# Decoder layer on one core: the first keys of cross-attention made earlier, the ranks behind the next queries

## The reference

```
x = layernorm(x + self_attention(x))        # 16 heads of 16; features normalised, then squared scores, causal
x = layernorm(x + cross_attention(x, ctx))  # 8 heads of 64, softmax over 1601 keys, output projection + bias
x = layernorm(x + experts(x))               # 8 experts, top 2 by softmax of a gate, silu(x w1) * (x w3) -> w2
```

## Time and profile before

| | us |
|---|---|
| median of 3 runs | 1288.47 |
| profiled execution | 1291.7 |
| its span, first to last instruction | 1290.0 |
| granted TensorE clock, mean | 0.97 |

### The profile page before, as it was taken

One profiled execution on the slowest core, in us unless ns is written; L12 is line 12 of the kernel. 1 busy time (PEld: TensorE's weight loads), 2 busy tenths in 40 slices (PEclk: granted clock), 3 DMA queues, 4 the chain that ended last, 5 costly groups with the idle time before them and its releaser, 6 DMA issues.

```text
span 1290.0 us, 18849 instructions
## 1 busy us (share of the span) xinstructions
PE 1172.4 (91%) x6456; PEld 685.7 (53%) x6456; DVE 725.9 (56%) x1297; ACT 592.1 (46%) x1031; POOL 715.3 (55%) x617
## 2 busy tenths in 40 slices
PE   3789797879999999999999999999999999999991
PEld 2456464545555555555555555555554466566661
DVE  7686867662466744657835556835665654423222
ACT  5676767624445643545543545444443423222222
POOL 2284656325587775678785776875766132422222
PEclk9899999979999999999999999999998999999996
DMA  6009700001000000100000100000003742332324
GB/s 200 17 9 337 254 2 1 1 1 26 1 1 1 26 1 2 42 1 1 26 34 1 43 1 26 9 26 17 1 1 130 262 103 43 74 45 46 47 37 143
DMA packets 38926, 65.75 MB, mean 51 GB/s; under 512 B 4129, under 2 KB 31393, under 8 KB 38561
## 3 DMA queue, kind: packets, MB, share of 16 engines
q1 hardware_dynamic: 25792, 49.45, 12.0%
q0 software_dynamic: 7152, 9.38, 4.4%
q10 hardware_dynamic: 5888, 5.72, 1.7%
HBM read 50.96 MB, written 30.61 MB: 63 GB/s over the span
## 4 chain that ended last, share of the span: by engine, by line
PE 74%; DVE 15%; issue 4%; ACT 4%; DMA 2%; ACTq 1%; another core or an unknown queue 0%; POOL 0%; SPq 0%; DVEq 0%; POOLq 0%
PE PS L1896 16%; PE PS L1907 12%; PE PS L1783 10%; PE PS L1973 9%; DVE mxp L1511 5%; PE PS L1991 5%; PE PS L1802 3%; PE PS L227 3%; PE PS L1694 2%; PE PS L1704 2%; PE PS L228 2%; PE PS L229 2%; PE PS L1683 2%; PE PS L1982 1%; PE PS L1877 1%
## 5 line engine op out<-in xcount | busy, mean ns | idle before, releaser
L732 POOL TENSOR_TENSOR acc<-acc,PX 128x1024 f32<-128x1024 f32 (+1 forms) x165 | 392.9, 2381 | 127.5 <-ACT PX L1012 118.8
L1012 ACT ACTIVATE PX<-PS 128x1024 f32<-128x1024 f32 (+1 forms) x208 | 212.5, 1026 | 261.9 <-PE PS L1896 256.3
L1511 DVE TENSOR_REDUCE mxp<-PS 128x2 f32<-128x804 f32 x256 | 243.1, 990 | 127.1 <-PE PS L1802 126.2
L1907 PE MATMUL PS<-PX,V 128*64 128x512 f32 (+1 forms) x832 | 209.4, 613 | 0.2 <-ACT PX L1012 0.2
L787 POOL DMA_INDIRECT Y<-yb,goal_u x39 | 60.8, 1558 | 183.6 <-DVE yb L1600 144.2
L1973 PE MATMUL PS<-W,XBT 128*128 x312 | 147.1, 594 | 1.6 <-issue 0.8
L664 POOL TENSOR_SCALAR_AFFINE_SELECT A<-A 128x128 f32<-128x128 f32 x256 | 85.4, 350 | 111.2 <-ACT A L899 108.3
L899 ACT ACTIVATE A<-PS 128x512 f32<-128x512 f32 (+3 forms) x256 | 97.7, 445 | 65.0 <-PE PS L1694 63.8
L1896 PE MATMUL PS<-QH,KH 64*128 64x512 f32 (+1 forms) x416 | 102.3, 488 | 4.8 <-ACT PX L1012 3.2
L1896 PEld LDWEIGHTS PS<-QH,KH 64*128 64x128 f32 (+1 forms) x416 | 38.1, 179 | 117.9 <-issue 81.3
L1907 PEld LDWEIGHTS PS<-PX,V 128*64 128x64 f32 (+1 forms) x832 | 48.6, 137 | 79.1 <-issue 73.2
(11 more groups left out here) (293 smaller groups left out, 2105.5 us busy)
## 6 DMA issues: line engine op xcount, KB each, us to landing
W<-in_w SPq DMA_DIRECT2D x24, 512.0 KB, 4.8
XB<-XG ACTq DMA_DIRECT2D x39, 130.0 KB, 2.1
X<-in_x SPq DMA_DIRECT2D x1, 2048.0 KB, 12.0
Y<-X SPq DMA_DIRECT2D x4, 512.0 KB, 3.4
X<-Y SPq DMA_DIRECT2D x4, 512.0 KB, 5.5
out<-X SPq DMA_DIRECT2D x8, 256.0 KB, 2.1
xt_raw<-in_xt SPq DMA_DIRECT2D x3, 512.0 KB, 3.9
c_raw<-in_ctxt SPq DMA_DIRECT2D x6, 200.0 KB, 2.7
```

The costliest lines, as they stand in the source:

```text
L732: ins = pool.tensor_tensor(sums[0:r], sums[0:r], PX[0:r, (NL * p + t) % NP, :, :], ALU.add)
L1012: act.activation(PX[0:r, u % NP, :, :], PS[0:r, score_buffer(u):score_buffer(u) + 2, :], ACT.Exp, scale=XD ** -0.5)\
L1511: dve.tensor_reduce(mxp[:, p % 2, :, v % NT, v // NT:v // NT + 1].rearrange("p a o -> p (a o)"), PS[:, k:k + 2, 0:BW], AX, ALU.max)\
L1907: mm = pe.matmul(PS[rows, 4, :], V[0:LROWS[j], j, P * p + XD * half:P * p + XD * half + XD], PX[0:LROWS[j], u % NP, half, :], start=(j == ...
```

## The change

The slots of the last batch are filled anew. Each entry of `MEANWHILE` is now three lists: for TensorE behind the second score, ahead of the value products, and behind them.

| step | slot before | slot after |
|---|---|---|
| xt 0, xt 1, q | 5, 6, 7 | 2, 3, 4 (ahead of the values) |
| k 0 to 3 | 9, 10, 11, 12 | 5, 6, 7, 8 |
| v 0 | 13 | 9 |
| max 0 to 11 | two each in 10 to 15 | two each in 9 to 14 |
| max 12 | handover | 15, behind the values |
| max 13 | handover, other banks | handover, banks 0 and 1 |

The context splits stay in slots 1 to 4. VectorE and ScalarE take the same steps in the new order; in slot 15 VectorE now copies the quad ahead of the maximum. The keys of pair 0 can no longer overlap the buffers that are live at slot 5, so high and low keys are laid out by parity of the pair: K0 (even pairs) over `c_first`, K1 (odd pairs) behind the queries, PX behind V. Since K0 lies over `c_first`, the keys of batch 0 wait for all four context splits. In `ROUTING` ranks and settle 0 move from (2, 12) to (3, 1), behind the next "q" and the pair's "total", "hout" and "ctx 3".

```diff
-        PX = sxx("PX", [P, NP, 2, T])
+        K0 = sxx("K0", [P, 2, L], f32r)
         QH, QL = sxx("QH", [P, 2, T], f32r), sxx("QL", [P, 2, T], f32r)
-        KH, KL = sxx("KH", [P, 2, L], f32r), sxx("KL", [P, 2, L], f32r)
+        K1 = sxx("K1", [P, 2, L], f32r)
+        KH, KL = ([K[:, part, :] for K in (K0, K1)] for part in range(2))
         unit = sxx("unit", [P, P], f32r)
         V = sxx("V", [P, NL, INNER])
+        PX = sxx("PX", [P, NP, 2, T])
...
-        sf("under_px", [P, 4096])
...
-                   (2, 12): [("ranks",), ("settle", 0)], (3, 2): [("settle", 1)], (3, 3): [("settle", 2)], (3, 4): [("settle", 3)],
+                   (3, 1): [("ranks",), ("settle", 0)], (3, 2): [("settle", 1)], (3, 3): [("settle", 2)], (3, 4): [("settle", 3)],
...
-        EARLY_MAX = 12
+        EARLY_MAX = 14
...
-        MEANWHILE = {n: [("ctx", n - 1)] for n in range(1, 1 + NB)}
-        MEANWHILE.update({5: [("xt", 0)], 6: [("xt", 1)], 7: [("q", 0)], 9: [("k", 0, 0)],
-                          10: [("max", 0, 0), ("k", 0, 1), ("max", 0, 1)], 11: [("max", 0, 2), ("k", 0, 2), ("max", 0, 3)],
-                          12: [("max", 0, 4), ("k", 0, 3), ("max", 0, 5)], 13: [("max", 0, 6), ("v", 0), ("max", 0, 7)],
-                          14: [("max", 0, 8), ("max", 0, 9)], 15: [("max", 0, 10), ("max", 0, 11)]})
-        HANDOVER = [("self", ("back", 3)), ("self", ("quad", 3)), ("cross", ("max", 0, 12)), ("cross", ("max", 0, 13)),
-                    ("self", ("yt", 1)), ("cross", ("max", 0, 14)), ("cross", ("max", 0, 15)), ("self", ("out", 0)),
-                    ("cross", ("mrow", 0))]
+        MEANWHILE = {1: ([("ctx", 0)], [], []), 2: ([("ctx", 1)], [("xt", 0)], []), 3: ([("ctx", 2)], [("xt", 1)], []),
+                     4: ([("ctx", 3)], [("q", 0)], []), 5: ([], [("k", 0, 0)], []), 6: ([], [("k", 0, 1)], []),
+                     7: ([], [("k", 0, 2)], []), 8: ([], [("k", 0, 3)], []),
+                     9: ([("max", 0, 0)], [("v", 0)], [("max", 0, 1)])}
+        MEANWHILE.update({n: ([("max", 0, 2 * n - 18)], [], [("max", 0, 2 * n - 17)]) for n in range(10, 15)})
+        MEANWHILE[15] = ([], [], [("max", 0, 12)])
+
+        HANDOVER = [("self", ("back", 3)), ("self", ("quad", 3)), ("cross", ("max", 0, 13)), ("self", ("yt", 1)),
+                    ("cross", ("max", 0, 14)), ("cross", ("max", 0, 15)), ("self", ("out", 0)), ("cross", ("mrow", 0))]
...
-                    if n == SLOTS - 1:
-                        for s in meanwhile(n, b):
-                            cross_step(0, s)
                     if n % NT == NT - 1:
                         quad_out(b, n // NT)
...
-                    pe.wait_ge(c_lo, 8 * b + 2 * s[2] + 2)
+                    pe.wait_ge(c_lo, 8 if b == 0 else 8 * b + 2 * s[2] + 2)
```

More of the change, by code:

```diff
@@ L518, in decoder_layer @@
             + [("turn " + part, g, q) for g, q in ((0, 0), (0, 1), (1, 0)) for part in "qk"]
-        MEANWHILE = {n: [("ctx", n - 1)] for n in range(1, 1 + NB)}
-        MEANWHILE.update({5: [("xt", 0)], 6: [("xt", 1)], 7: [("q", 0)], 9: [("k", 0, 0)],
-                          10: [("max", 0, 0), ("k", 0, 1), ("max", 0, 1)], 11: [("max", 0, 2), ("k", 0, 2), ("max", 0, 3)],
-                          12: [("max", 0, 4), ("k", 0, 3), ("max", 0, 5)], 13: [("max", 0, 6), ("v", 0), ("max", 0, 7)],
-                          14: [("max", 0, 8), ("max", 0, 9)], 15: [("max", 0, 10), ("max", 0, 11)]})
-        HANDOVER = [("self", ("back", 3)), ("self", ("quad", 3)), ("cross", ("max", 0, 12)), ("cross", ("max", 0, 13)),
-                    ("self", ("yt", 1)), ("cross", ("max", 0, 14)), ("cross", ("max", 0, 15)), ("self", ("out", 0)),
-                    ("cross", ("mrow", 0))]
+        MEANWHILE = {1: ([("ctx", 0)], [], []), 2: ([("ctx", 1)], [("xt", 0)], []), 3: ([("ctx", 2)], [("xt", 1)], []),
[6 more added lines that the diff above has]
+                    ("cross", ("max", 0, 14)), ("cross", ("max", 0, 15)), ("self", ("out", 0)), ("cross", ("mrow", 0))]
         def meanwhile(n, b):
-            return MEANWHILE.get(n, []) if b == B - 1 else []
+            return MEANWHILE.get(n, ([], [], [])) if b == B - 1 else ([], [], [])
         def started(b, n, least):
@@ L909, in attention @@
                         step(b + d, s)
-                    for s in meanwhile(n, b):
+                    for s in sum(meanwhile(n, b), []):
                         cross_step(0, s)
@@ L977, in cross_step @@
                     lo, hi = BEDGE[s[2]], BEDGE[s[2] + 1]
-                    act.copy(KH[:, s[1] % 2, lo:hi], PS[:, misc_bank(b, s), lo - BSTART[s[2]]:hi - BSTART[s[2]]]).then_inc(misc_hi, 1)
+                    act.copy(KH[s[1] % 2][:, lo:hi], PS[:, misc_bank(b, s), lo - BSTART[s[2]]:hi - BSTART[s[2]]]).then_inc(misc_hi, 1)
                 if kind == "v":
@@ L1274, in attention @@
                             step(b + d, s)
-                    if n != SLOTS - 1:
-                        for s in meanwhile(n, b):
-                            cross_step(0, s)
+                    for s in sum(meanwhile(n, b), []):
+                        cross_step(0, s)
             for s in OPENING:
@@ L1528, in cross_step @@
                     lo, hi = BEDGE[s[2]], BEDGE[s[2] + 1]
-                    dve.tensor_tensor(KL[:, s[1] % 2, lo:hi], PS[:, misc_bank(b, s), lo - BSTART[s[2]]:hi - BSTART[s[2]]],
-                                      as32(KH[:, s[1] % 2, lo:hi]), ALU.subtract).then_inc(misc_ok, 1)
+                    dve.tensor_tensor(KL[s[1] % 2][:, lo:hi], PS[:, misc_bank(b, s), lo - BSTART[s[2]]:hi - BSTART[s[2]]],
+                                      as32(KH[s[1] % 2][:, lo:hi]), ALU.subtract).then_inc(misc_ok, 1)
                 if kind == "wo":
@@ L1756, in attention @@
                     half = (len(steps) + 1) // 2
-                    others = [s for s in meanwhile(n, b) if s[0] != "ctx"]
+                    mid, between, end = meanwhile(n, b)
                     for j in range(4):
@@ L1765, in attention @@
                                 step(b + d, s)
-                            for s in others[:1]:
+                            for s in mid:
                                 cross_step(0, s)
-                    for s in others[1:2]:
+                    for s in between:
                         cross_step(0, s)
@@ L1773, in attention @@
                         step(b + d, s)
-                    for s in others[2:]:
+                    for s in end:
                         cross_step(0, s)
@@ L1802, in row_maxima @@
                     mm = pe.matmul(bank(bk + half, BW), QH[rows, p % 2, P * i:P * i + P],
-                                   KH[rows, p % 2, BSTART[k]:BSTART[k] + BW], start=True, stop=True)
+                                   KH[p % 2][rows, BSTART[k]:BSTART[k] + BW], start=True, stop=True)
                 mm.then_inc(mx_mm, 1)
@@ L1894, in scores_t @@
                     for half, rows in heads(p):
-                        lhs = one_row[rows, 0:r] if k_ is one_row else k_[rows, p % 2, keys]
+                        lhs = one_row[rows, 0:r] if k_ is one_row else k_[p % 2][rows, keys]
                         mm = pe.matmul(bank(score_buffer(u) + half, rows=r), lhs, q_[rows, p % 2, :], start=(n == 0), stop=(n == 3))
```

## The result

The changed kernel takes 1300.88 us in the median of 5 runs (1297.1 to 1303.09), against 1288.47 before (5 runs beside it, 1286.63 to 1291.5): a ratio of 1.0093, 95% interval 1.0068 to 1.0118. It is 12 us slower; 2.8 were forecast, with 1295.5 as the upper end. Its profiled execution took 1303.09 us, span 1301.3. It ran the same 18849 instructions.

What follows compares the result with a forecast made beforehand. TensorE was taken as the bound, busy 1172.4 of 1290.0 us. Part 1 +1.3, the crossings' waits +0.9 and their clock +0.6 gave +2.8 us on the median 1288.5, so 1291.3; range 1285.0 to 1295.5.

Steps and rivals of the forecast that it cites:

- the clock's share of the sum: Time added by a lower TensorE clock: none in self-attention's last batch, +0.6 us at the two crossings.
- Part 1, up to slot 10: Self-attention's last batch, slots 2 to 9: 5.1 us more work and 2.4 net waits, so slot 10 begins 7.5 us later.
- the four waits: New TensorE waits in slots 2 to 9: queries 0.9, first keys 2.8, last key chunk 1.0, first maximum 1.4 us.
- Sum 4.7 + 1.2 = 5.9 won: From slot 10: 4.7 us of work moved out and 1.2 less in the last slot and its wait before the handover's transpose.
- the 5.9 and 0.3 of the forecast: Gains from slot 10 on (5.9 us) and in the handover with one maximum fewer (0.3 us).
- rival 3: Slots 10 to 15 and handover: clock falls before slot 14; batch +4.7 us, with crossings +8.0, median 1296.5; chance 0.17.
- Part 1 at equal clock: Self-attention's last batch and handover: +7.5 − 5.9 − 0.3 = +1.3 us.
- Part 2, the steps: Crossings: queries start at +3.7 after mrow, ranks wait 2.2 us, keys start at +15.2; +1.2 and −0.3, sum +0.9 us.
- Part 2, the clock: Crossings: even odds that the new waits (2.2 and 1.0 us) once slow six matmuls by 0.2 us each; +0.6 us.
- the 0.7 of the forecast: Crossings: VectorE's subtraction ahead of pos takes 0.7 us, not held up by GpSimd.

Runs made afterwards that it cites:

- e11: Changed kernel with ranks ahead of the split at (2, 12), unused matmuls ahead of maxima from 2 on and 9 ahead of the first keys; ratio 0.9969 to before.
- e7: Kernel before with ranks ahead of slot (2, 12)'s context split and 2 unused matmuls ahead of each of maxima 8 to 15; ratio 0.9928 to before.
- e6: Kernel before with 2 unused matmuls ahead of each of maxima 8 to 15; ratio 1.0003 to before.
- e4: Changed kernel with 36 unused matmuls ahead of maxima from 2 on and 8 ahead of the ranks at both crossings; ratio 1.0031 to before.
- e2: Kernel before with only ranks and settle 0 moved to (3, 1); ratio 1.0020 to before.
- e3: Changed kernel with 36 unused matmuls ahead of the maxima from number 2 on; ratio 1.0053 to before.
- e5: Kernel before with ranks and settle 0 still at (2, 12) but ahead of that slot's context split; ratio 0.9956 to before.
- e1: Changed kernel with ranks put back to (2, 12), so the new slots only; ratio 1.0057 to before.

## Why the prediction was wrong

The step that failed is the clock's share of the sum: nothing in the batch, and 0.6 us at the crossings.

*Part 1, up to slot 10: right, in part by luck.* Slot 10 began 7.7 us later by the length of the first window, 7.5 forecast. TensorE's work there grew by 5.0 us for 5.1 forecast; the four waits were forecast at 0.9, 2.8, 1.0 and 1.4 and came at 0.78, 2.46, 0.95 and 1.36. But the first keys ran at the lower clock behind their long wait: the chunk took 1.97 us, where the forecast had 1.01. With the clock at 1.00 from there on (e11) slots 0 to 10 take 42.7 instead of 44.1 us, so at full clock the delay is about 6.4.

*Part 1, slots 10 to 15: wrong.* The step "Sum 4.7 + 1.2 = 5.9 won" took durations from rows at full clock. The stretch gave back 2.0. From the transposes in slot 10 to the second scores the kernel before takes 40.2 us, the changed one 40.0, and e11, at a clock of 1.00, 34.1: the 5.9 and 0.3 of the forecast were there, and the clock took them. Before, the two parts of that stretch ran at 0.90 and 0.68:

```profile
253.17:280.74 27.57, 20.04 (x125) 10.85 (x124) 17.19 (x25) 9.47 (x25) 6.71 (x27) 0.90 0.00 1
280.74:293.36 12.62, 10.95 (x53) 8.21 (x53) 6.79 (x12) 3.50 (x4) 2.86 (x6) 0.68 0.01 3
```

It is the mechanism of rival 3, a clock that falls once keys and values no longer stand between the maxima: "It decides if the clock is at its lower level before 270 us", and it fell at 270. Its size was short too: 4.7 for the batch against 7.5 measured, since the handover ran at 0.50 throughout and so did half of the second "out" behind it.

*Part 1 at equal clock: about right.* The forecast was +1.3. e11 takes 0.9 more than e7 and 1.7 more than e6, each with some unused matmuls of its own. The clocks are not quite equal: e6 and e7 had 0.89 ahead of slot 10, and e7 0.94 behind it, where e11 had 1.00. So this holds to 1 or 2 us, and e11's whole time does not show it.

*Part 2, the steps: right.* Queries at +3.7, ranks behind 2.2 us of wait, keys at +15.2 (measured +15.78 and +15.41, the excess at low clock). For waits alone +1.2 was forecast at the second crossing and −0.3 at the third; e4's third crossing at full clock is 1.1 over the second and 0.4 under the third of before.

*Part 2, the clock: wrong.* "I give the new waits (2.2 and 1.0) even odds of doing this once, for the 6 × 0.2 us that it cost there: +0.6." It happened at both crossings, and lasted over the ranks or a set of scores, the keys and their value products, not over six matmuls. Against e4's 44.7 that is 1.9 us at the second crossing and 2.8 at the third.

So the mis-sized term is the clock's. The batch and the two crossings grew by 12.9 us in the profiles. Of these, 1.3 and 0.9 are what the forecast had for waits; about 6 in the batch (7.5 less 1.3) and about 4.5 at the crossings (5.4 less 0.9) come with the lower clock. These are sums of parts of two traces, good to 2 us, and up to 1.6 of the 4.5 is the luck of the 43.6; by the ratio of e2 the ranks cost 2.6 in all. That the clock is the cause in these stretches is shown by e3, e4 and e11, which add work and take less time there at a clock read as 1.00; e4 shows it for the whole time too. The rule of the Trainium skill (TensorE: Matmul & The Clock Gate, "What's actually happening"), that low activity lowers this clock and activity releases it, agrees with the 0.66 and 0.50 that became 1.00. It was given a chance of 0.17. It deserved more: the 0.55 of the handover showed that a part of the program with maxima and no keys loses its clock, and the change made exactly such a part longer.

The subtraction that stands ahead of "pos" was not held up by GpSimd: 0.69 us at both crossings. So the 0.7 of the forecast was right.

## What to carry to other kernels

In this kernel the work that stood between short waits also kept TensorE's clock up (0.92 in slots 10 to 15 with keys and values among the maxima, 0.66 without). When such work is moved away, price what remains at half speed, unless a row shows the clock high with so many gaps. And the wait that was taken from the queries went to the next steps that use the same bank: in such a chain look for the place where the reader of the bank has least ahead of it in its queue (e5), not for a later place. Where one trace has a stretch at full clock, look at the same stretch in another kernel that shares its program before counting on it.

## What was not expected of the hardware

The granted clock could be bought back with unused matmuls at a profit: 36 of them made the batch 4.4 us shorter (e3), and 9 made slots 0 to 10 shorter by 1.3 to 2.7 (e11). The profit isn't sure: 16 of them in the kernel before made its batch 1.4 us shorter and its time no shorter (e6). With the same program and nearly the same gaps the clock was not the same each time: at the second crossing a wait of 2.31 us left it at full speed in the kernel before, 2.33 and 2.32 us did not in e1 and e6, and in e4 one of two crossings with equal filling ran at 0.92, the other at 1.00.
